# Row and key scores of an attention block issued as four 32-column matmuls each

## The chip, the core and the metric

The kernel runs on one core of a Trainium2 chip. The core has a matrix engine (PE, with its weight loads listed as PEld), a vector engine (DVE), a scalar engine (ACT), GpSimd (POOL), a queue engine for transfers (SP), and 16 DMA engines. The metric is the device time of the whole program in microseconds. Each time below is a median of runs or comes from one profiled execution.

## What is computed

One transformer block in float32: layer norm, attention with 16 heads of 8 dimensions over 8 sequences of 512 tokens, a residual, a second layer norm, and a feed-forward part with one shared and eight routed experts (two per token). The part that matters here is the attention:

```python
q = (x @ Wq.T + bq).reshape(b, s, HEADS, HEAD_DIM)        # b=8, s=512, 16 heads of 8
k = (x @ Wk.T + bk).reshape(b, s, HEADS, HEAD_DIM)
attn = jnp.einsum('bqhd,bkhd->bhqk', q, k) / np.sqrt(HEAD_DIM)
attn = jax.nn.softmax(attn, axis=-1) * head_mask[None, :, None, None]
out = jnp.einsum('bhqk,bkhd->bqhd', attn, v).reshape(b, s, HIDDEN)
```

## The kernel before

Heads are taken in groups of four (`hg`, 4 groups; `j` is the head in the group), and sequences in a loop (`b`, 8 of them: the first and the last are written out, the six between are a hardware loop). q and k are kept as bfloat16 parts, three for each value, so that a product of parts gives float32 accuracy. This is why a score contracts over 72 part rows and more, though a head has 8 dimensions.

Scores are computed twice. **Row scores** (`row_scores`, L1147) put 128 queries on PSUM partitions and 512 keys along the free axis. DVE takes the maximum over the keys of two such tiles at once (L792, four PSUM banks, so PE may be two pairs ahead). The maxima are split into parts and transposed by PE (`max_rows`, L1191), copied by ACT (L630) and sent by a small DMA (L314) into two extra rows of `q_op`. **Key scores** (`key_scores`, L1165) put 128 keys on partitions and 512 queries along the free axis. Their contraction runs over 128 rows, and the two extra rows subtract the maximum of each query. ACT takes the exponential of a whole tile (L643) into `probs`. The key scores have two banks (four in the last two groups of heads), so the key score of step n waits for the exponential of step n-2.

**The product** of probabilities and values (`pv`, L1176) follows 11 steps behind. It takes one tile of 128 keys at a time: four matmuls in float32, one for each head, each with 32 columns of weights and 512 queries. Head `j` writes PSUM partitions 32j to 32j+31 of one bank. In the trace a float32 matmul is two records, so a `pv` shows as 8 matmul records. It is the only place where the 128 columns of PE are used as four tiles of 32.

A group of heads has 16 steps `s`. Step s issues its key score (K) and zero to two row scores (R) of the group after next (`ROW_TILES`). With four steps to a `pv`, PE's order repeats as

K R, K R R, K R, K, pv

Four such periods make a group of heads, 16 a sequence and 128 the attention. Other work of PE is put in between at fixed steps: `max_rows` after step 7 of each group, the output projection of the sequence before (`project_out`, L1202, once each after steps 0 to 3 of group 1), a transpose of the normalised rows (L1215, group 2), the router (L1221, group 3) and the ranks of the routed tokens (L1232 to L1239, group 3). All of these use weights of 128 columns. After the attention, the experts take the rest of the time, from about 510 us on.

DVE has its own order: the maximum of a row pair, and between them the transposes and the norm of the group's output, the residual, statistics and routing.

## Time and profile before

| | us |
|---|---|
| time, median of 3 runs | 732.31 (731.01 to 732.35) |
| span of the profiled execution, first to last instruction | 730.6 |
| PE busy in it | 653.3 |
| DVE busy | 551.8 |
| ACT busy | 440.2 |
| one iteration of the loop over sequences (of the seven after b = 0) | about 55 |

The busy time of an engine is the time in which at least one of its instructions is recorded as running. PE's matmuls overlap: a matmul of 512 columns in bfloat16 is recorded with 380 ns, while the next one starts 220 ns after it. So the distance between the starts says what a matmul costs, and the recorded length adds the way through the array. A timeline row can merge several instructions (x8); its start is that of the first and its length reaches to the end of the last. An arrow in brackets names what ended the idle time before a row. "Idle" is only counted where no instruction of the engine is recorded. K stands for a row of L1165, R for one of L1147, and pv for one of L1176.

### The profile page before, as it was taken

The page shows a single profiled execution, that of the slowest core. Times are in us where ns is not written, and L with a number is a line of the kernel's source. Part 1 is how long each engine was busy: PE and PEld are TensorE (multiplying, and loading weights), DVE is VectorE, ACT ScalarE, POOL GpSimd, SP SyncE. Part 2 cuts the span into 40 slices and gives each one's busy share as a digit, 9 for nine tenths or more (in the row PEclk, how much of TensorE's full clock was granted, in tenths as well). Part 3 has the DMA queues.
Part 4 walks back from the last instruction along what each step waited for, and adds up shares of the span by engine and source line. Part 5 has one row for each costly group of instructions (what it writes and reads, how often), then busy time and mean ns, then how long its engine had stood idle before and what let it go on. Part 6 is the DMA issues. An engine that isn't in the chain of part 4 may idle for free.

```text
span 730.6 us, 15017 instructions
## 1 busy us (share of the span) xinstructions
PE 653.3 (89%) x3976; PEld 330.0 (45%) x3976; DVE 551.8 (76%) x1252; ACT 440.2 (60%) x953; POOL 241.6 (33%) x314
## 2 busy tenths in 40 slices
PE   2866899999899899899899899898788999999996
PEld 1531222332233223223223223223578999999965
DVE  6989799999699698698698698663165666666658
ACT  0870577786586586587587487486524555555541
POOL 6767000022221211311311310413374455545541
PEclk9995799999999899999999899899998999999999
DMA  5499575212112112212112212100022222222164
GB/s 144 123 333 322 132 187 167 49 51 59 51 42 64 54 33 71 56 33 69 58 33 69 58 33 57 37 2 17 14 59 63 67 65 65 65 65 65 47 224 137
DMA packets 67592, 61.04 MB, mean 84 GB/s; under 512 B 16250, under 2 KB 58106, under 8 KB 67562
## 3 DMA queue, kind: packets, MB, share of 16 engines
q1 hardware_dynamic: 63242, 51.79, 25.8%
q0 software_dynamic: 4320, 8.89, 3.6%
q8 instruction: 14, 0.23, 0.1%
q14 instruction: 16, 0.13, 0.1%
HBM read 35.76 MB, written 24.62 MB: 83 GB/s over the span
## 4 chain that ended last, share of the span: by engine, by line
PE 64%; DVE 11%; issue 9%; POOL 3%; ACT 1%; another core or an unknown queue 1%; DMA 1%; DVEq 0%; SPq 0%; ACTq 0%; POOLq 0%
PE ps L1165 14%; PE ps L1176 13%; PE ps L1147 11%; PE ps L1350 10%; PE ps L1362 9%; DVE mx L792 5%; POOL slots L501 2%; DVE x_sb L1090 2%; PE ps L1302 1%; PE ps L1310 1%; PE ps L1340 1%; PE ps L1202 1%; PE ps L1221 1%; ACT probs L643 1%
## 5 line engine op out<-in xcount | busy, mean ns | idle before, releaser
L643 ACT ACTIVATE probs<-ps 128x512 f32<-128x512 f32 x512 | 281.3, 595 | 131.1 <-PE ps L1165 105.4
L792 DVE TENSOR_REDUCE mx<-ps 128x2 f32<-128x1024 f32 x256 | 306.4, 1213 | 50.7 <-PE ps L1147 39.0
L1165 PE MATMUL ps<-q_op,k_op 128*128 128x512 bf16 x512 | 199.5, 396 | 21.3 <-issue 14.2
L1147 PE MATMUL ps<-k_op,q_op 96*128 96x512 bf16 x512 | 187.8, 406 | 14.9 <-DVE mx L792 9.5
L1165 PEld LDWEIGHTS ps<-q_op,k_op 128*128 128x128 bf16 x512 | 50.1, 99 | 205.1 <-ACT probs L643 140.5
L1176 PE MATMUL ps<-probs,v_op 128*32 128x512 f32 x1024 | 141.2, 626 | 0.0
L690 ACT ACTIVATE probs<-ps,b_cur 128x128 f32<-128x128 f32 x284 | 81.4, 368 | 73.7 <-PE ps L1350 54.9
L501 POOL DMA_INDIRECT slots<-route_sb,slot_u x64 | 66.5, 1038 | 119.5 <-DVE slot_u L884 102.4
L544 POOL DMA_INDIRECT results<-rest,row_id x71 | 73.3, 1032 | 73.6 <-DVE rest L1034 55.8
L1147 PEld LDWEIGHTS ps<-k_op,q_op 96*128 96x128 bf16 x512 | 50.2, 101 | 68.9 <-DVE mx L792 34.3
L1350 PE MATMUL ps<-xn,qk 128*128 128x128 f32 x568 | 79.5, 284 | 1.4 <-ACT probs L690 1.1
L1362 PE MATMUL ps<-k_op,probs 128*128 128x128 f32 x568 | 75.2, 275 | 0.0
L1350 PEld LDWEIGHTS ps<-xn,qk 128*128 128x128 f32 x568 | 70.5, 195 | 6.2 <-ACT probs L690 5.3
L1362 PEld LDWEIGHTS ps<-k_op,probs 128*128 128x128 f32 x568 | 69.2, 192 | 0.2 <-issue 0.2
L465 POOL COPY v_op<-v_all 128x128 f32 (+1 forms) x32 | 9.3, 309 | 89.6 <-PE ps L1176 89.6
L473 POOL TENSOR_TENSOR mean_d<-stats 128x4 f32<-128x4 f32 x8 | 1.6, 202 | 110.1 <-DVE stats L841 110.1
L811 DVE STREAM_TRANSPOSE o_t<-ps 128x512 f32<-128x512 f32 x32 | 22.7, 708 | 19.5 <-remote 11.0
L1176 PEld LDWEIGHTS ps<-probs,v_op 128*32 128x32 f32 x1024 | 20.6, 109 | 36.4 <-issue 29.0
L1027 DVE COPY xn<-ps 128x128 f32<-128x128 f32 x71 | 20.6, 290 | 21.6 <-PE ps L1340 14.0
L1034 DVE TENSOR_TENSOR rest<-ps,b_sb 128x128 f32<-128x128 f32 x71 | 20.2, 284 | 21.5 <-PE ps L1362 21.5
L669 ACT ACTIVATE probs<-ps,b_sb 128x512 f32<-128x512 f32 x32 | 21.1, 689 | 22.4 <-PE ps L1302 19.9
L1310 PEld LDWEIGHTS ps<-w_sb,probs 128*128 128x128 f32 x256 | 31.1, 201 | 2.1 <-issue 1.9
(135 smaller groups left out, 623.5 us busy)
## 6 DMA issues: line engine op xcount, KB each, us to landing
q_op<-q_scr SPq DMA_DIRECT2D x96, 96.0 KB
k_op<-k_scr SPq DMA_DIRECT2D x96, 96.0 KB
w_sb<-in_W SPq DMA_DIRECT2D x18, 256.0 KB, 4.4
probs<-slots SPq DMA_DIRECT2D x71, 64.5 KB
k_scr<-probs SPq DMA_DIRECT2D x16, 256.0 KB, 3.2
q_scr<-probs SPq DMA_DIRECT2D x8, 384.0 KB, 3.0
k_scr<-probs SPq DMA_DIRECT2D x8, 384.0 KB, 3.5
k_scr<-probs SPq DMA_DIRECT2D x16, 128.0 KB, 3.0
```

The costliest lines, as they stand in the source:

```text
L501: nc.gpsimd.indirect_dma_start(slots, bass.IndirectOffsetOnAxis(slot_u[:, K2 * i + k:K2 * i + k + 1], 0), y2[:, i, k, :], None).then_inc(s ...
L544: nc.gpsimd.indirect_dma_start(results, bass.IndirectOffsetOnAxis(row_id[:, v, h:h + 1], 0), r_tile[:, v, h, :], None).then_inc(s_res[v], 16)
L643: nc.scalar.activation(probs[:, i, j, :], ps[:, BK_S + j % key_banks(b, hg), :], ACT.Exp, scale=float(D) ** -0.5).then_inc(s_exp, 1)
L690: nc.scalar.activation(hid_tile[:, par, c, :], ps[:, BK_TU + 2 * par + c // 2, TR * (c % 2):TR * (c % 2 + 1)], ACT.Gelu_apprx_tanh, bias=b ...
L792: nc.vector.reduce_max(mx[:, slot % 2, 2 * p:2 * p + 2], ps[:, bank:bank + 2, :], AX.X).then_inc(s_max, 1)
L811: nc.vector.transpose(o_t[:, :, :].rearrange("p a c -> p (a c)"), ps[:, BK_O, :]).then_inc(s_ot, 1)
L1147: last = nc.tensor.matmul(ps[:, BK_A + a % 4, :], q_op[hg][0:SH, j, P * i:P * (i + 1)], k_op[hg][0:SH, j, :], start=True, stop=True)
L1165: nc.tensor.matmul(ps[:, BK_S + j % key_banks(b, hg), :], k_op[hg][:, j, P * i:P * (i + 1)], q_op[hg][:, j, :], start=True, stop=True).the ...
L1176: last = nc.tensor.matmul(ps[32 * j:32 * j + 32, BK_O, :], v_op[:, hg, i, j, :], probs[:, i, j, :], start=(i == 0), stop=(i == NT - 1))
L1310: last = nc.tensor.matmul(ps[:, DN0 + b % 2, C * i:C * (i + 1)], hid[:, b % 2, c, P * i:P * (i + 1)], w2_sb[:, E, c, :], start=(c == 0), s ...
L1350: last = nc.tensor.matmul(ps[:, BK_TU + 2 * par + c // 2, TR * (c % 2):TR * (c % 2 + 1)], w1_cur[:, v, P * c:P * (c + 1)], yT_tile[:, par, ...
L1362: last = nc.tensor.matmul(ps[:, BK_TD + par, C * h:C * (h + 1)], hid_tile[:, par, c, P * h:P * (h + 1)], w2_cur[v][:, c, :], start=(c == 0 ...
```

## The change

Both kinds of scores are issued as four matmuls in place of one. Each takes 32 of the 128 weight columns and writes 32 PSUM partitions of the same bank; all four read the same moving operand of 512 columns. Nothing else changes: the waits stand before the first of the four, the semaphore is raised by the last, and the order of the steps is as it was.

```diff
@@ row_scores
-                last = nc.tensor.matmul(ps[:, BK_A + a % 4, :], q_op[hg][0:SH, j, P * i:P * (i + 1)], k_op[hg][0:SH, j, :],
-                                        start=True, stop=True)
+                for c in range(P // 32):
+                    last = nc.tensor.matmul(ps[32 * c:32 * c + 32, BK_A + a % 4, :],
+                                            q_op[hg][0:SH, j, P * i + 32 * c:P * i + 32 * c + 32], k_op[hg][0:SH, j, :],
+                                            start=True, stop=True)
                 if a % 2:
                     last.then_inc(s_sa, 1)
@@ key_scores
-                nc.tensor.matmul(ps[:, BK_S + j % key_banks(b, hg), :], k_op[hg][:, j, P * i:P * (i + 1)], q_op[hg][:, j, :],
-                                 start=True, stop=True).then_inc(s_sb, 1)
+                for c in range(P // 32):
+                    last = nc.tensor.matmul(ps[32 * c:32 * c + 32, BK_S + j % key_banks(b, hg), :],
+                                            k_op[hg][:, j, P * i + 32 * c:P * i + 32 * c + 32], q_op[hg][:, j, :],
+                                            start=True, stop=True)
+                last.then_inc(s_sb, 1)
```

The 1,024 score matmuls (512 row, 512 key) become 4,096, each with a weight load of its own. Lines behind the first edit move down by two to five in the changed kernel (L1147 to L1148, L1165 to L1168, L1176 to L1181, L1191 to L1196, L1202 to L1207).

PE in the loop over sequences, from the last key score of group 0 on: the `pv` behind it, and the first steps of group 1 with the output projections (ps is PSUM; REGISTER_ALU and ISA rows compute the value of a wait). Before:

```order
L1165 MATMUL ps<-q_op,k_op 128x512
L1176 MATMUL ps<-probs,v_op 32x512 x4
L209 ISA
L1165 MATMUL ps<-q_op,k_op 128x512
L209 ISA
L1147 MATMUL ps<-k_op,q_op 128x512
L1202 MATMUL ps<-wo_sb,o_sb 128x128
L1165 MATMUL ps<-q_op,k_op 128x512
L1147 MATMUL ps<-k_op,q_op 128x512 x2
L1202 MATMUL ps<-wo_sb,o_sb 128x128
```

After:

```order
L1168 MATMUL ps<-q_op,k_op 32x512 x4
L1181 MATMUL ps<-probs,v_op 32x512 x4
L209 ISA
L1168 MATMUL ps<-q_op,k_op 32x512 x4
L209 ISA
L1148 MATMUL ps<-k_op,q_op 32x512 x4
L1207 MATMUL ps<-wo_sb,o_sb 128x128
L1168 MATMUL ps<-q_op,k_op 32x512 x4
L1148 MATMUL ps<-k_op,q_op 32x512 x8
L1207 MATMUL ps<-wo_sb,o_sb 128x128
```

Every row of scores is now a row of four 32-column matmuls (or eight, where two row scores follow each other), in the same place. Before, the `pv` was the only 32-column work between 128-column rows. Now the projections are the only 128-column work between 32-column rows.

The same engine, later in group 1, around step 7 with the transpose of the maxima. Before:

```order
L1165 MATMUL ps<-q_op,k_op 128x512
L1147 MATMUL ps<-k_op,q_op 128x512
L209 REGISTER_ALU
L1165 MATMUL ps<-q_op,k_op 128x512
L1191 MATMUL ps<-id_bf,mx_parts 128x128
L1171 REGISTER_ALU
L1176 MATMUL ps<-probs,v_op 32x512 x4
```

After:

```order
L1168 MATMUL ps<-q_op,k_op 32x512 x4
L1148 MATMUL ps<-k_op,q_op 32x512 x4
L209 REGISTER_ALU
L1168 MATMUL ps<-q_op,k_op 32x512 x4
L1196 MATMUL ps<-id_bf,mx_parts 128x128
L1176 REGISTER_ALU
L1181 MATMUL ps<-probs,v_op 32x512 x4
```

The transpose (L1191, now L1196) keeps its 128 columns and stands between the key score of step 7 and the `pv`, both of which have 32-column tiles now.

## Rows read from the trace of the kernel before

**Rows 1.** The page: the chain that ended last, shares by engine

```profile
PE 64%; DVE 11%; issue 9%; POOL 3%; ACT 1%; another core or an unknown queue 1%; DMA 1%; DVEq 0%; SPq 0%; ACTq 0%; POOLq 0%
```

**Rows 2.** Timeline of PE: start us, us, engine line op out<-in xcount

```profile
311.18 0.39 PE L1165 MATMUL ps<-q_op,k_op 128*128 128x512 bf16 x1
312.28 0.38 PE L1165 MATMUL ps<-q_op,k_op 128*128 128x512 bf16 x1
312.50 0.38 PE L1147 MATMUL ps<-k_op,q_op 96*128 96x512 bf16 x1
312.75 0.39 PE L1165 MATMUL ps<-q_op,k_op 128*128 128x512 bf16 x1
313.07 1.07 PE L1176 MATMUL ps<-probs,v_op 128*32 128x512 f32 x8
314.06 0.39 PE L1165 MATMUL ps<-q_op,k_op 128*128 128x512 bf16 x1
```

**Rows 3.** Timeline of ACT beside it, same columns

```profile
311.61 2.18 ACT L643 ACTIVATE probs<-ps 128x512 f32<-128x512 f32 x4 [0.63 <-PE ps L1165]
```

**Rows 4.** Timeline of PE: the last three products, back to back

```profile
503.34 2.78 PE L1176 MATMUL ps<-probs,v_op 128*32 128x512 f32 x24
```

**Rows 5.** The page's costliest groups: weight loads (PEld) of scores and product

```profile
L1165 PEld LDWEIGHTS ps<-q_op,k_op 128*128 128x128 bf16 x512 | 50.1, 99 | 205.1 <-ACT probs L643 140.5
L1176 PEld LDWEIGHTS ps<-probs,v_op 128*32 128x32 f32 x1024 | 20.6, 109 | 36.4 <-issue 29.0
```

**Rows 6.** Timeline of PE: an output projection between scores, and a transpose before a product

```profile
304.71 0.39 PE L1202 MATMUL ps<-wo_sb,o_sb 128*128 128x128 f32 x2
304.94 0.38 PE L1165 MATMUL ps<-q_op,k_op 128*128 128x512 bf16 x1
310.03 0.22 PE L1191 MATMUL ps<-id_bf,mx_parts 128*128 128x128 bf16 x1
310.18 1.07 PE L1176 MATMUL ps<-probs,v_op 128*32 128x512 f32 x8
```

**Rows 7.** Timeline of DVE in b = 4: rows with idle time

```profile
308.57 0.69 DVE L834 TENSOR_TENSOR x_sb<-ps,x_sb 128x512 f32 x1 [0.54 <-PE ps L1202]
318.53 1.23 DVE L792 TENSOR_REDUCE mx<-ps 128x2 f32<-128x1024 f32 x1 [0.39 <-PE ps L1147]
321.41 2.36 DVE L792 TENSOR_REDUCE mx<-ps 128x2 f32<-128x1024 f32 x2 [0.36 <-PE ps L1147]
330.52 1.23 DVE L792 TENSOR_REDUCE mx<-ps 128x2 f32<-128x1024 f32 x1 [0.72 <-PE ps L1147]
334.17 1.23 DVE L792 TENSOR_REDUCE mx<-ps 128x2 f32<-128x1024 f32 x1 [0.87 <-PE ps L1147]
```

**Rows 8.** Windows: stretch, its length, busy time (x instructions) of each engine

```profile
303.27:358.39 55.12, 50.93 (x292) 16.34 (x291) 46.22 (x79) 38.30 (x74) 12.38 (x23) 0.97 0.21 53
310.18:313.07 2.89, 2.89 (x19) 0.79 (x17) 2.89 (x8) 2.26 (x6) 0.00 (x0) 1.00 0.02 3
347.76:354.38 6.62, 3.40 (x19) 0.79 (x17) 3.10 (x5) 2.03 (x5) 5.10 (x6) 0.93 0.16 51
354.38:358.39 4.01, 4.01 (x18) 0.92 (x17) 2.48 (x5) 2.64 (x5) 0.47 (x2) 0.69 0.05 16
```

**Rows 9.** L1176 by source: duration ns min/median/max, single pvs, then three in a row

```profile
L1176 PE MATMUL ps<-probs,v_op x24: 592/604/617, 310.2 to 316.9; 128*32 128x512 f32 x24
L1176 PE MATMUL ps<-probs,v_op x24: 592/592/617, 503.3 to 505.5; 128*32 128x512 f32 x24
```

**Rows 10.** Windows, same columns: b = 0, and the last two groups of heads

```profile
109.89:133.37 23.48, 23.48 (x131) 6.39 (x130) 21.23 (x27) 17.61 (x35) 0.31 (x1) 1.00 0.51 141
484.14:503.30 19.16, 18.01 (x120) 5.38 (x119) 6.11 (x28) 18.11 (x38) 0.92 (x3) 1.00 0.01 1
```

**Rows 11.** DMA: instruction queue 8 (packets, MB, share), and a small transfer

```profile
q8 instruction: 14, 0.23, 0.1%
q_op<-mxT SPq DMA_DIRECT2D x64, 4.0 KB, 1.7
```

## The prediction

> **What bounds the kernel now.** The chain that ended last lies on PE for 64% [rows 1], and the table above has PE busy for 653.3 of 730.6 us, DVE for 551.8. Recorded matmuls overlap, so I went on to PE's timeline and read distances between starts. One period of the attention (eight scores and a pv) runs from the pv at 310.18 to the one at 313.07, 2.89 us [rows 2, 6]. Its parts:
> - pv to the first key score K0: 0.99 (313.07 to 314.06).
> - K0 to the last key score K3, seven scores: 1.57 (311.18 to 312.75).
> - K3 to pv: 0.32.
> - One score elsewhere costs 0.22 (312.28 to 312.50).
>
> Seven scores at 0.22 would be 1.54. K3 comes at 1.57 because it waits until the exponential of K1 has freed its bank: ACT starts 0.43 after K0 and runs four exponentials in 2.18, one behind the other [rows 3], so the second ends about 1.1 later, and 0.43 + 1.1 is K3's time.
>
> Then DVE: in 55.12 us, one iteration of the loop, it is busy for 46.22 [rows 8]. Of the 8.9 idle us about 5.0 lie in two windows (3.10 busy of 6.62, 2.48 of 4.01), where all engines stand still for a while (PE is busy for 3.40, ACT for 2.03 of the 6.62) and PE's granted clock falls behind it (0.93 and 0.69 on average, a mix of the levels 2.4 and 1.2 GHz) [rows 8]. Outside them DVE is over 90% busy, in places (the window from 310.18) without a gap [rows 8]. So PE and DVE take turns as the bound, and what PE gains is worth no more than DVE's idle time before a maximum or the residual: 0.54, 0.39, 0.36, 0.72, 0.87 and smaller ones [rows 7].
>
> **What the change removes: two turns of PE's shape per period.** K3 to pv takes 0.10 more than a score's 0.22. What a pv costs among its own kind is in the last three pvs, which follow each other: 24 records in 2.78 against 8 in 1.07, so (2.78 - 1.07)/4 = 0.43 for each of its two passes, 0.86 a pv [rows 4, 6]. In the period it holds PE for 0.99, 0.13 more. Going into and out of 32-column tiles thus costs 0.10 + 0.13 = 0.23 a period. With scores in the same tiles both go.
>
> The Trainium skill ("TensorEngine Tiling (Array Packing)", Tiling Modes) says that changing the tiling mode drains the engine, while changing the tile within a mode does not. The trace agrees, with the 0.10 and 0.13 above. By its sentence alone the change is a plain gain on PE.
>
> **What a tiled score costs.** No row shows a bfloat16 score in 32-column tiles. Lower bound: the 0.22 of a full one. Upper bound: the four run one after another, 0.88. The nearest row is pv, with the same four tiles: a pass takes 0.43 [rows 4], twice the 0.22 of bfloat16, as a float32 pass should if all four tiles run at once. Its operands need 512 x 4 bytes in 0.43 for each tile and partition, which is the rate of 512 x 2 in 0.22. What speaks for more is that records of single pvs are 592 or 617 ns long, half of each [rows 9]: a first pass takes 0.025 longer, a weight load that nothing hides. In the three pvs in a row the median is the minimum, 592, so it is paid once and not six times [rows 9]. Tiled scores follow each other in the same way. I take 0.22, and keep 0.22 + 0.025, about 0.25, for the range. ACT starts when the last of the four tiles is done, which I put at 0.02 later (an estimate from the same 0.025): K0 to K3 becomes 1.59.
>
> There are 3,072 more weight loads. One of 32 columns is recorded with 109 ns against 99 for a full one in bfloat16 [rows 5], and four of them are unseen beneath a pass of 0.43. Four beneath 0.22 is twice that rate.
>
> The Trainium skill ("TensorEngine Tiling (Array Packing)", Restrictions) says that column tiling disables the fast weight load, which speaks against the change. By "TensorE: Matmul & The Clock Gate" (LDWEIGHTS) a load takes its columns divided by 1.2 GHz; four of 32 are an estimated 0.107 us, still under 0.22. By the rule a score would cost more only where its load is exposed.
>
> **A plain period afterwards:** pv to K0 0.86, K0 to K3 1.59, K3 to pv 0.22. That is 2.67 for 2.89 (the parts of before sum to 2.88), so -0.21.
>
> **What the change adds: turns around 128-column work.** A projection between scores costs nothing but itself now (304.71 to 304.94, 0.23) [rows 6]. Afterwards it stands between tiled scores and pays both turns, +0.23. The same holds for the transposes and the router (one block each), whose periods come out even: +0.23 - 0.21. In a period with a max_rows, score to transpose is a new turn (+0.10), transpose to pv stays (0.15) [rows 6], pv to K0 gains 0.13: about even. Three projections fall in one period.
>
> **One iteration, followed on DVE.** DVE works without a gap until about 308.0, then waits for the fourth projection (0.54 idle) [rows 7]. While DVE has no gap it holds PE, and I take this to hide the first of the three projections between scores; the other two pay +0.46, K3 to pv gives 0.10 back: **+0.36**. From 309.3 to 318.1 DVE is the bound: 0. From 318 to 334 the idle times above are DVE waiting for row scores, 2.34 in the last four of [rows 7]. PE's lead grows by 0.23 at the first pv, 0.21 at four more and 0.02 at the one behind a max_rows, and loses 0.23 in two insertions: **-0.63**, which the gaps can take as it builds up. From 334 to 344 DVE is the bound again: 0. In the slow-clock stretch DVE is idle for 1.5 of 4.01 [rows 8]. No row prices a turn at the low clock; between 0.23 (the same) and 0.46 (twice), one and a half periods save 0.35 to 0.69. I take the lower end, as K3 there waits for ACT: **-0.35**. Sum -0.6. Six such iterations: **-3.7**.
>
> b = 0 with the group behind it has no inserts but max_rows: 16 periods, of which 12 save 0.21, -2.5. DVE is idle for 2.25 of the second half's 23.48 [rows 10] and as much in the first, so nearly all of it is taken: **-2.3**. The last sequence has no further row scores in its last two groups, and there ACT is busy 18.11 of 19.16 [rows 10]: 0. Its first two groups have the projections (+0.36) and some plain periods: **-0.5**. The row scores before 77 us and the experts: 0 (DVE and loads bound the first; the second is untouched).
>
> Sum -6.5: the profiled 730.6 becomes 724.1. The median lies 1.7 above that span, and becomes **725.8** (732.31 - 6.5).
>
> **Rivals.** (1) *DVE takes it.* If the gaps shrink less than I counted (another maximum is late, ACT is next), the six iterations give 0 and b = 0 gives -1: 731.3. For: DVE over 90% busy. Against: each gap is released by PE.
> (2) *Slower: the loop's code.* PE's loop body grows by 384 matmuls and 384 loads; one iteration now has 292 and 291 records [rows 8], so it becomes about 2.3 times as long. The instruction queue moved 14 packets of 16 KB [rows 11], and its share of 0.1% of 16 engines is some 11.7 us, 0.8 each; a small transfer takes 1.7 from issue to landing [rows 11]. If the longer body no longer stays in the engine, each of six jumps back waits 1.7 to 2.5 us for its first block: +10 to +15, less 6.5: 736 to 741. It decides once the body is larger than what is kept. Nothing in the rows shows where that is.
> The Trainium skill ("Runtime: NRT & Kernel Launch", Instruction fetch mechanics) gives PE room for 2,048 instructions in blocks of 256; the new body is some 1,470 by count, so it should fit, unless the blocks fetched ahead push its start out.
> (3) *Slower: loads or tiles in line.* If each tiled score costs 0.25, a period is 7 x 0.25 + 0.25 + 0.90 = 2.90 and nothing is gained, while eleven insertions an iteration (four max_rows, four projections, one each of transposes, router and ranks) pay 0.23 each. With DVE's own stretches hiding two thirds of these 2.5 us, that leaves +0.8, six times: 737. For: the 0.025 above, and the doubled rate of loads. Against: it appears once in three pvs.
> (4) *Much slower: no overlap* in bfloat16 or with one shared moving operand, 0.88 a score: +0.66 x 1,024, less DVE's slack, over 1,300 us. The rate of pv speaks against it.
>
> **How the numbers follow.** Chances: forecast 0.57, (1) 0.15, (2) 0.13, (3) 0.12, (4) 0.03. The forecast's own range is 719 to 729: at its low end twice the gain is taken (-13), at its high end half. The range must leave out no more than two in ten: 718 to 738 leaves out (4), the longer half of (2), and a little at both ends. A measurement of this kernel tells 0.2% (1.5 us) from no change. Faster by more: the forecast and a part of (1), 0.61. Within: 0.13. Slower: (2), (3), (4) less what they leave, 0.26.
>
> **What would show it.** In the profile after: distances of 0.22 from the first record of a score to that of the next (0.25 for rival 3), 0.22 from K3 to pv, 0.86 from pv to K0, a plain period of 2.67; projections 0.23 dearer; DVE's idle rows shorter, its busy share up. Rival 2 shows as idle PE right behind the jump back, once an iteration, and more packets on queue 8. I am wrong if weight loads are exposed at every score, or if the standstill once an iteration grows with PE's number of instructions.

## The result: slower by 2.4%, and the profile after

The changed kernel takes 749.37 us (median of 4 runs, 748.18 to 750.9) where the kernel before, measured beside it, takes 732.33 (731.01 to 733.71). The ratio is 1.024, 95% interval 1.021 to 1.028. The forecast was 725.8, with a range up to 738: the sign is wrong. The profiled execution spans 748.8 us where that of before spans 730.6.

The page of the kernel after, engines with busy time and number of instructions, then the chain that ended last and the instruction queue, as in [rows 1, 11]:

```profile
PE 649.5 (87%) x7048; PEld 351.7 (47%) x7048; DVE 551.4 (74%) x1252; ACT 440.4 (59%) x953; POOL 241.9 (32%) x314
...
q8 instruction: 23, 0.38, 0.2%
...
PE 58%; DVE 12%; issue 10%; POOL 3%; ACT 2%; another core or an unknown queue 2%; DMA 1%; DVEq 0%; SPq 0%; ACTq 0%; POOLq 0%
```

PE has 3,072 instructions more and is busy for 3.8 us less. The span grew by 18.2 us, so PE stands idle for longer.

Timeline of PE in the kernel after, the period that answers to [rows 2, 6] (start us, us, engine line op out<-in xcount):

```profile
320.08 0.23 PE L1196 MATMUL ps<-id_bf,mx_parts 128*128 128x128 bf16 x1
320.24 1.07 PE L1181 MATMUL ps<-probs,v_op 128*32 128x512 f32 x8
321.12 0.40 PE L1168 MATMUL ps<-q_op,k_op 128*32 128x512 bf16 x4
321.34 0.40 PE L1148 MATMUL ps<-k_op,q_op 96*32 96x512 bf16 x4
...
322.70 0.40 PE L1168 MATMUL ps<-q_op,k_op 128*32 128x512 bf16 x4
322.93 1.03 PE L1181 MATMUL ps<-probs,v_op 128*32 128x512 f32 x8
```

Here the forecast holds to within two hundredths of a microsecond. From the product to the first score there are 0.88 us, where it had 0.86, between two scores 0.22 (a group of four tiles moves on at the rate of one full-width matmul), from K0 to K3 1.58, from K3 to the product 0.23, and the period is 2.69 for 2.89, where it had 2.67.

Windows of the kernel after, columns as in [rows 8] (length, busy time and instructions of PE, PEld, DVE, ACT, POOL, then clock, DMA share, GB/s): one iteration of the loop, a plain period, and the two periods around the standstill.

```profile
312.54:370.48 57.94, 50.94 (x678) 18.93 (x674) 46.23 (x79) 38.37 (x74) 12.37 (x23) 0.94 0.20 50
320.24:322.93 2.69, 2.69 (x42) 1.09 (x45) 2.69 (x8) 2.06 (x6) 0.00 (x0) 1.00 0.02 3
...
357.95:367.44 9.49, 4.40 (x41) 1.09 (x44) 4.00 (x6) 3.01 (x6) 5.11 (x6) 0.68 0.13 43
367.44:370.48 3.04, 3.04 (x44) 0.97 (x40) 2.06 (x4) 1.96 (x5) 0.00 (x0) 0.88 0.00 0
```

The iteration takes 57.94 us where it took 55.12. The period with the standstill takes 9.49 us where it took 6.62 [rows 8]. PE works for 4.40 of them, at a granted clock of 0.68, a mix of the levels 2.4 and 1.2 GHz. In its fifth pair of numbers POOL is busy for 5.11 us, where the plain period has 0.00.

What every engine does there, in both kernels. Timelines of PE, ACT and POOL in the kernel before (in brackets the idle time just before):

```profile
348.76 0.39 PE L1165 MATMUL ps<-q_op,k_op 128*128 128x512 bf16 x1
...
352.44 0.39 PE L1165 MATMUL ps<-q_op,k_op 128*128 128x512 bf16 x1 [2.42 <-issue]
...
351.79 0.60 ACT L643 ACTIVATE probs<-ps 128x512 f32<-128x512 f32 x1 [3.19 <-remote]
353.19 0.60 ACT L643 ACTIVATE probs<-ps 128x512 f32<-128x512 f32 x1 [0.80 <-PE ps L1165]
...
344.58 1.10 POOL L501 DMA_INDIRECT slots<-route_sb,slot_u  x1 [14.03 <-DVE slot_u L884]
345.98 0.96 POOL L501 DMA_INDIRECT slots<-route_sb,slot_u  x1 [0.30 <-issue]
...
353.57 0.96 POOL L501 DMA_INDIRECT slots<-route_sb,slot_u  x1 [0.30 <-issue]
```

And in the kernel after:

```profile
356.40 0.39 PE L1168 MATMUL ps<-q_op,k_op 128*32 128x512 bf16 x4
...
357.45 0.40 PE L1168 MATMUL ps<-q_op,k_op 128*32 128x512 bf16 x4 [0.45 <-issue]
...
360.37 0.40 PE L1168 MATMUL ps<-q_op,k_op 128*32 128x512 bf16 x4 [1.36 <-issue]
360.60 0.39 PE L1148 MATMUL ps<-k_op,q_op 96*32 96x512 bf16 x4
364.62 0.62 PE L1168 MATMUL ps<-q_op,k_op 128*32 128x512 bf16 x4 [3.63 <-issue]
...
359.72 0.60 ACT L643 ACTIVATE probs<-ps 128x512 f32<-128x512 f32 x1 [2.32 <-remote]
363.97 0.60 ACT L643 ACTIVATE probs<-ps 128x512 f32<-128x512 f32 x1 [3.65 <-remote]
364.46 0.25 ACT L630 ACTIVATE mxT<-ps 32x128 bf16<-32x128 bf16 x1
...
354.02 1.10 POOL L501 DMA_INDIRECT slots<-route_sb,slot_u  x1 [13.82 <-DVE slot_u L884]
...
363.00 0.96 POOL L501 DMA_INDIRECT slots<-route_sb,slot_u  x1 [0.30 <-issue]
```

POOL issues the eight indirect scatters of put_rows, one every 1.26 us, 9.95 us in all. Some 4 us behind the first of them (3.4 in the kernel after) ACT begins to wait for key scores that PE's own record shows as done. In a free period an exponential starts 0.04 us behind the recorded end of its score (311.18 + 0.39, then 311.61) [rows 2, 3]. In the kernel before, the score of 348.76 ends at 349.15 and its exponential starts at 351.79, 2.6 us later. In the kernel after, the score of 356.40 ends at 356.79 and its exponential starts at 359.72, 2.9 us later; the score of 357.45 ends at 357.85, and its exponential starts at 363.97, 6.1 us later and just behind the last scatter (363.00 + 0.96).

Which exponential belongs to which score follows from the order of the program. A score waits for the exponential two scores back, as those of 352.44 and 364.62 do here, and the copy L630 at 364.46 stands right behind the exponential of step 7. PE in turn waits for these exponentials. So the standstill reads as a wait for PE's completion signals while POOL issues scatters, and time is already lost in the first sequence that has scatters beside it. That is a reading of two timelines; the runs below test it.

### The profile page after: what moved, and what is told of

Read it like the earlier page. It is cut to its first block, busy times and chain, and to the rows that moved or that the text cites. A ratio compares the mean times of both kernels' runs of the same rounds, so it can differ in the third digit from the quotient of the medians.

```text
span 748.8 us, 21161 instructions
## 1 busy us (share of the span) xinstructions
PE 649.5 (87%) x7048; PEld 351.7 (47%) x7048; DVE 551.4 (74%) x1252; ACT 440.4 (59%) x953; POOL 241.9 (32%) x314
## 3 DMA queue, kind: packets, MB, share of 16 engines
q0 software_dynamic: 4320, 8.89, 3.6%
## 4 chain that ended last, share of the span: by engine, by line
PE 58%; DVE 12%; issue 10%; POOL 3%; ACT 2%; another core or an unknown queue 2%; DMA 1%; DVEq 0%; SPq 0%; ACTq 0%; POOLq 0%
PE ps L1168 12%; PE ps L1148 10%; PE ps L1181 10%; PE ps L1355 10%; PE ps L1367 8%; DVE mx L792 6%; POOL slots L501 2%; DVE x_sb L1090 2%; ACT probs L643 2%; PE ps L1207 2%; PE ps L1307 1%; PE ps L1315 1%; PE ps L1345 1%; PE ps L1226 1%
## 5 line engine op out<-in xcount | busy, mean ns | idle before, releaser
L1168 PE MATMUL ps<-q_op,k_op 128*32 128x512 bf16 x2048 | 205.7, 397 | 39.4 <-issue 24.4
L1148 PE MATMUL ps<-k_op,q_op 96*32 96x512 bf16 x2048 | 194.4, 408 | 18.6 <-DVE mx L792 13.0
L1181 PE MATMUL ps<-probs,v_op 128*32 128x512 f32 x1024 | 136.4, 610 | 0.0
L1168 PEld LDWEIGHTS ps<-q_op,k_op 128*32 128x32 bf16 x2048 | 54.9, 96 | 165.5 <-ACT probs L643 91.6
L1148 PEld LDWEIGHTS ps<-k_op,q_op 96*32 96x32 bf16 x2048 | 55.2, 99 | 111.8 <-DVE mx L792 63.9
L501 POOL DMA_INDIRECT slots<-route_sb,slot_u x64 | 66.4, 1038 | 118.1 <-DVE slot_u L884 101.0
L1181 PEld LDWEIGHTS ps<-probs,v_op 128*32 128x32 f32 x1024 | 29.7, 111 | 14.7 <-issue 3.3
```

The lines of the kernel that those rows point to most:

```text
L501: nc.gpsimd.indirect_dma_start(slots, bass.IndirectOffsetOnAxis(slot_u[:, K2 * i + k:K2 * i + k + 1], 0), y2[:, i, k, :], None).then_inc(s ...
L1148: last = nc.tensor.matmul(ps[32 * c:32 * c + 32, BK_A + a % 4, :], q_op[hg][0:SH, j, P * i + 32 * c:P * i + 32 * c + 32], k_op[hg][0:SH, j ...
L1168: last = nc.tensor.matmul(ps[32 * c:32 * c + 32, BK_S + j % key_banks(b, hg), :], k_op[hg][:, j, P * i + 32 * c:P * i + 32 * c + 32], q_op ...
L1181: last = nc.tensor.matmul(ps[32 * j:32 * j + 32, BK_O, :], v_op[:, hg, i, j, :], probs[:, i, j, :], start=(i == 0), stop=(i == NT - 1))
```

## The experiments

Theory A: while POOL issues indirect DMAs one behind the other, PE gets only so many instructions completed (or their signals passed on), so the standstill grows with PE's number of instructions there. Rivals: B, column tiling costs time by itself; C, the scatters have no part in it; D, the faster stream of tiles arrives in another phase. Each run stood beside runs of the kernel before, from which its ratio comes. Where a run leaves the scatters out, its text on record says so. "Iteration" is the stretch of [rows 8, first row] in that kernel's own trace, from the second product of b = 4 to that of b = 5.

| run | us, median | ratio, 95% interval | iteration, us |
|---|---|---|---|
| before | 732.33 | | 55.12 |
| after | 749.37 | 1.024 (1.021 to 1.028) | 57.94 |
| e1 before, no scatters | 689.59 | 0.940 (0.937 to 0.944) | 50.21 |
| e2 after, no scatters | 687.85 | 0.939 (0.935 to 0.943) | 50.13 |
| e3 full-width in group 0 | 733.16 | 1.001 (0.998 to 1.003) | 56.56 |
| e4 before, halves | 746.82 | 1.019 (1.014 to 1.023) | 59.93 |
| e5 two tiles of 64 | 760.35 | 1.039 (1.036 to 1.041) | 61.73 |
| e6 before, spaced | 698.36 | 0.954 (0.951 to 0.956) | 50.22 |
| e7 after, spaced | 701.46 | 0.957 (0.953 to 0.961) | 50.92 |
| e8 before, plain DMAs | 690.99 | 0.944 (0.942 to 0.947) | 50.21 |
| e9 before, POOL adds | 699.57 | 0.957 (0.952 to 0.962) | 51.03 |
| e10 tiled in group 0 only | 748.91 | 1.024 (1.020 to 1.028) | 58.03 |
| e11 before, two bursts | 711.01 | 0.972 (0.968 to 0.976) | 53.10 |
| e12 spaced, tiles in b = 0 | 698.48 | 0.955 (0.950 to 0.959) | 50.2 |
| e13 before, 24 plain DMAs | 696.50 | 1.010 (1.008 to 1.011), see below | 50.2 |
| e14 after, spaced by 4 | 707.69 | 1.025 (1.023 to 1.027), see below | 54.06 |
| e15 after, again | 750.63 | 1.025 (1.020 to 1.030) | 58.27 |
| e16 as e13, again | 704.49 | 0.961 (0.957 to 0.965) | 50.2 |

Each set of runs had one chip to itself. In five sets the medians of the kernel before lay between 732.1 and 733.5 us; in the set of e13 and e14 it took 689.73 (7 runs, 688.9 to 691.05). That set is a finding of its own, told at its place.

The iterations of one trace differ where there is a standstill, so the last column is one sample. Taken from the row numbers of one sequence to those of the next (slot_u on DVE, the rows that the scatters wait for), the first five take 55.1 to 56.3 us in the kernel before (mean 55.7), 58.0 to 59.9 after (58.8), 55.1 to 56.6 in e3 (55.7), 58.0 to 58.5 in e10 (58.2), 55.5 to 59.8 in the halves (58.2) and 58.9 to 61.9 in e5 (61.1). Without the scatters they agree to 0.03.

**Is it the scatters? (e1, e2)**

```diff
-                for i in range(NT):
-                    for k in range(K2):
-                        nc.gpsimd.indirect_dma_start(slots, bass.IndirectOffsetOnAxis(slot_u[:, K2 * i + k:K2 * i + k + 1], 0),
-                                                     y2[:, i, k, :], None).then_inc(s_put, 16)
+                pool.sem_inc(s_put, 16 * NC)
```

> The kernel before, without the indirect scatters of the loop (put_rows raises its semaphore and issues nothing; the experts' tiles and the results are then read from rows written elsewhere, in the same number and size, so this part of the computation is left out). Theory A (PE's completion signals are passed on late while GpSimd issues the eight scatters, and the standstill of group 0 is that lateness): the standstill goes in the kernel before already. The two periods around it took 6.62 and 4.01 us where a plain one takes 2.89, so 4.8 us an iteration and, with the low clock behind it, 5 to 6: six of them take 730.6 to about 700 (695 to 706). Theory C (the standstill is owed to something else at that place, the shift copies, the loads or the loop's own code): 728 to 732, with the standstill where it was.

> The changed kernel without the same scatters (left out as in the run before it). Theory A: no standstill, so the tiles' own gain is left, 0.2 us in each plain period: below the kernel before without scatters by 6 to 10 us, some 690 to 696. Theory B (column tiles cost time by themselves at some places, with or without GpSimd at work): above the kernel before without scatters, by 10 us or more. Theory C: about 749, with the longer standstill.

Windows of e1, an iteration and the period that held the standstill, then the same of e2:

```profile
288.31:338.52 50.21, 49.24 (x292) 16.18 (x291) 46.00 (x79) 38.06 (x74) 4.53 (x15) 1.00 0.18 48
332.75:335.63 2.88, 2.88 (x18) 0.78 (x16) 2.66 (x4) 2.29 (x6) 0.00 (x0) 1.00 0.02 3
```

```profile
283.63:333.76 50.13, 48.66 (x679) 18.98 (x674) 46.10 (x79) 38.03 (x74) 4.53 (x15) 1.00 0.19 48
328.38:331.07 2.69, 2.69 (x42) 1.09 (x44) 2.49 (x3) 2.10 (x6) 0.00 (x0) 1.00 0.02 3
```

Theory C falls, and A had put e1 at 695 to 706, so more comes back than it counted. Without the scatters neither kernel has a standstill, and PE's clock stays at 1.00. The period that took 6.62 and 9.49 us takes 2.88 and 2.69. In spans of the profiled executions the scatters cost the kernel before 41.2 us (730.6 - 689.4) and the changed one 65.2 (748.8 - 683.6), 24.0 more. That overstates the growth: the profiled run of e1 is the longest of its four and that of e2 the shortest, and 4.3 of the 5.8 us between them lie ahead of the first row numbers (1.3 are a single wait for a copy's DMA in b = 0 that the profile of e1 has and that of e2 does not). From the row numbers of the first sequence to those of the seventh, the four traces take 327.2 us (before), 345.9 (after), 293.6 (e1) and 293.1 (e2). There the scatters cost 33.6 and 52.8 us, so the standstills grew by 19.3, and the tiles gained 0.6.

By medians the changed kernel is 17.0 us slower with the scatters and 1.7 us faster without them, and the medians of e1 and e2 cannot be told apart. So theory A's "6 to 10 us below" for e2 was too much. B falls for the loop: with 678 instructions for 292 an iteration takes 50.13 for 50.21.

Part of the 41 us lies behind the loop, where POOL issues its last scatters (L501 has 2% of the chain that ended last, on the page of before): from the last product to the end e1 takes 218 us and the kernel before 227.

**Which scores matter? (e3, e10)** Row scores of group 2 and key scores of group 0 are those issued in group 0 of a sequence, where the scatters run.

```diff
-                for c in range(P // 32):
+                w = P if hg == 2 else 32
+                for c in range(P // w):
```

This is row_scores of e3, with w for 32 in the lines below it; key_scores has `hg == 0`. In e10 the two widths are exchanged.

> The changed kernel, but the scores that are issued in group 0 of each sequence (row scores of group 2, key scores of group 0) are full-width as before; groups 1 to 3 are tiled. Theory A: in group 0, where the scatters run, PE has the instruction count of the kernel before, so the standstill is that of before (6.6 and 4.0 us in the two periods), while 48 of 64 periods keep the gain of 0.2 us where PE bounds them: 724 to 729. Theory B (the tiles themselves): between the two kernels, 740 to 746. Theory D (the faster stream of PE ahead of group 0 moves it against the scatters, and the phase makes the stall long): 745 or more, with the long standstill.

> The changed kernel with tiles only for the scores that are issued in group 0 of each sequence, where the scatters run; groups 1 to 3 are full-width as before. Theory A: group 0 alone carries the loss, so the long periods are those of the changed kernel (9.5 to 10.7 us and the one behind it 3 to 4.7), in spite of 48 of 64 periods being those of before: 745 to 752. Rival D (the stream of tiles ahead of group 0 decides): 730 to 736.

A quarter of the tiles carries the whole loss: e10 has them only beside the scatters and takes 748.91, the time of the changed kernel. e3 has them everywhere else and is within the noise of the kernel before (its 56.56 in the table is one of its long iterations; their mean is that of before). D falls with e10, B with e3. Theory A's 724 to 729 for e3 missed too: the tiles outside group 0 gain nothing that shows.

**Tiles, or the number of instructions? (e4, e5)**

```diff
-                last = nc.tensor.matmul(ps[:, BK_A + a % 4, :], q_op[hg][0:SH, j, P * i:P * (i + 1)], k_op[hg][0:SH, j, :],
-                                        start=True, stop=True)
+                for c in range(2):
+                    last = nc.tensor.matmul(ps[:, BK_A + a % 4, 256 * c:256 * c + 256], q_op[hg][0:SH, j, P * i:P * (i + 1)],
+                                            k_op[hg][0:SH, j, 256 * c:256 * c + 256], start=True, stop=True)
```

This is row_scores of e4; its key scores are cut alike. e5 is the changed kernel with 64 in the place of 32.

> The kernel before with every row and key score cut in two along its moving axis (two full-width matmuls of 256 columns each instead of one of 512): the same product with twice the score instructions and no column tiling. Theory A (number of instructions): the standstill grows by about a third of what four tiles add to it (one instruction more for each score where the tiles add three), so 735 to 742. Theory B (column tiling): 730 to 733, with the standstill of before, unless the second load of the weights shows (a load is 0.10 us beside 0.11 us of columns, so it should just be hidden).

> The changed kernel with two column tiles of 64 for each score instead of four of 32: the number of instructions of the halves (two for each score), as column tiles. Theory A (the standstill grows with PE's number of instructions, whatever their shape): the long periods of group 0 are those of the halves, 9.5 to 10.5 us, and the time is theirs, 747, or down to 742 for what shorter turns of shape give back. Theory B (four tiles in flight together are dear by themselves): about halfway from the kernel before to the halves or better, 733 to 740.

The halves use no column tiles at all, and the kernel before becomes 1.9% slower by them. The window with their standstill:

```profile
352.71:363.22 10.51, 3.90 (x27) 1.71 (x25) 3.48 (x6) 3.02 (x6) 5.54 (x7) 0.72 0.12 39
```

Their plain period still takes 2.89, so the loss is in group 0 again. The text of A missed its size: it put the growth at about a third of what the tiles add (735 to 742), and it is 13.7 us (746.82 against 733.10 beside it) where the tiles add 17.0, with twice the instructions of a score instead of four times. How PE stands in the last 6.44 us of the eight scatters shows what may be behind it. The groups of PE's matmuls there, by line (busy us, mean ns, idle before; the number of instructions is the x), in the kernel before (348.08 to 354.53), in the halves (353.02 to 359.46) and in the kernel after (357.52 to 363.96):

```profile
L1176 PE MATMUL ps<-probs,v_op 128*32 128x512 f32 x12 | 2.1, 757 | 0.0
L1165 PE MATMUL ps<-q_op,k_op 128*128 128x512 bf16 x4 | 1.8, 442 | 3.2 <-issue 3.2
L1147 PE MATMUL ps<-k_op,q_op 96*128 96x512 bf16 x4 | 1.4, 380 | 0.0
```

```profile
L1180 PE MATMUL ps<-probs,v_op 128*32 128x512 f32 x8 | 1.1, 605 | 0.0
L1148 PE MATMUL ps<-k_op,q_op 96*128 96x256 bf16 x6 | 1.0, 272 | 0.0
L1167 PE MATMUL ps<-q_op,k_op 128*128 128x256 bf16 x4 | 0.8, 278 | 1.5 <-issue 1.5
```

```profile
L1181 PE MATMUL ps<-probs,v_op 128*32 128x512 f32 x8 | 1.1, 604 | 0.0
L1168 PE MATMUL ps<-q_op,k_op 128*32 128x512 bf16 x8 | 0.8, 390 | 1.8 <-issue 1.8
L1148 PE MATMUL ps<-k_op,q_op 96*32 96x512 bf16 x4 | 0.4, 381 | 0.0
L1196 PE MATMUL ps<-id_bf,mx_parts 128*128 128x128 bf16 x1 | 0.2, 230 | 0.0
```

20, 18 and 21 matmuls (and 21 in e5 and in e10): PE gets through nearly the same number in the same time, whatever one of them is worth. That is some 4 for each scatter, where the windows of a free plain period count 19 in 2.89 us before [rows 8] and 42 in 2.69 after. These 20 hold eight scores in the kernel before, five in the halves, three in the kernel after. The same stretch of the other rows of scatters gives 20, 18 and 21 again in the four inner ones of the six up to 503 us; the first and the last of them let 28 to 33 through, and e3, full-width there, has 15 to 24 in the inner ones. The number is the same only in this stretch: over the whole row, 9.95 us, it is 38, 44 and 61, since 22, 30 and 44 pass in the first 3.5 us (matmuls under way at the boundary are counted on both sides). So "more instructions, longer standstill" is what the runs show; a fixed number for each scatter is a reading of one stretch.

The lateness can outlast the scatters. In the halves ACT starts the exponential of a score that ended at 354.16 only at 361.17, 7.0 us later and 1.7 us behind the end of the last scatter (358.50 + 0.96). That the halves, already stopped until then, leave four tiles little more to lose would explain why the two are so close; no run tests it.

e5 is slower than either, 760.35, where theory A had put it at 742 to 747. Its standstill (365.94 to 375.79, 9.85 us) is that of the others. Of the 3.8 us that its iteration has on that of the changed kernel, 2.1 are in the one period behind the standstill (5.14 us for 3.04), for which no cause was looked for. Most of the rest is in the other groups: a plain period takes 2.92, so tiles of 64 remove no turn of shape next to a product in tiles of 32, and the period with the projections takes 4.47 us (4.24 in the changed kernel, 3.66 before). A single mode for both was needed for the gain that the change has.

**Is it the transfers, the descriptors, or any work of POOL? (e8, e9)**

```diff
-                        nc.gpsimd.indirect_dma_start(slots, bass.IndirectOffsetOnAxis(slot_u[:, K2 * i + k:K2 * i + k + 1], 0),
-                                                     y2[:, i, k, :], None).then_inc(s_put, 16)
+                        nc.gpsimd.dma_start(slots[E * REGION - P * (K2 * i + k + 1):E * REGION - P * (K2 * i + k), :],
+                                            y2[:, i, k, :]).then_inc(s_put, 16)
```

That is e8. In e9 there stands in the place of the loop over the scatters:

```diff
+                for n in range(NC - 2):
+                    nc.gpsimd.tensor_tensor(busy_sb[:, n, :, :], y2[:, :, 0, 0:C], y2[:, :, 1, 0:C], ALU.add).then_inc(s_put, 16)
```

> The kernel before with the eight indirect scatters replaced by eight plain DMAs of the same rows to fixed rows, issued on GpSimd's queue too (the rows are not put at their slots, and experts' tiles and results are read from rows written elsewhere, in the same number and size; that part of the computation is left out). Theory P (what holds PE's signals is GpSimd making descriptors, for any DMA of its queue): a standstill of the kernel before in group 0, 720 to 733. Theory Q (it needs the indirect form, in which GpSimd reads 128 row numbers and makes 128 destinations): no standstill, 688 to 697.

> The kernel before with six additions of 512 columns on GpSimd, one behind the other, in the place of the eight scatters (that part of the computation is left out; the experts' tiles and the results are read from rows written elsewhere, in the same number and size). An addition of that size took GpSimd 1.27 us in the kernel before, so it is at work for 7.6 us without a pause. Theory A (it is the making of indirect DMAs on GpSimd that holds PE's signals): no standstill, every iteration 50.2 us as without scatters, 688 to 693. Rival G (any long stretch of GpSimd's work holds them): the long periods of group 0 come back, 715 or more.

In e8 the queue moves what it did before (4,320 packets, 8.89 MB in both pages), and the iteration takes 50.21: the transfers are innocent. POOL worked on the eight for 4.39 us, which is only just as long as it took until ACT's gap began in the kernel before, so e8 alone cannot tell the indirect form from any DMA of that queue. In e9 POOL adds without a pause for 6.35 us. Windows of e9, its iteration, and the periods ahead of and behind 334.12:

```profile
288.86:339.89 51.03, 49.24 (x292) 16.20 (x291) 46.80 (x79) 38.06 (x74) 10.83 (x21) 1.00 0.19 47
330.10:334.12 4.02, 3.07 (x19) 0.94 (x18) 4.02 (x5) 2.19 (x5) 4.02 (x5) 1.00 0.31 64
334.12:337.00 2.88, 2.88 (x18) 0.78 (x16) 2.65 (x4) 2.29 (x6) 2.19 (x3) 1.00 0.02 3
```

The period of the standstill is back at 2.88, so a busy POOL alone does not hold PE. The 0.8 us in the period ahead (4.02 for 3.20 in e1) have another cause: DVE's small subtraction L806 took 0.98 us there beside POOL's additions, where its median is 166 ns. Theory A's 688 to 693 missed. The rest of the 10 us above e1 is mostly POOL's additions behind the loop (from the last product to the end, 225 us for 218). Whether it takes the indirect form, or any DMA of that queue in a long enough row, took two more sets (e13 to e16, below).

**Does a pause help? (e6, e7, e11, e12)**

```diff
                     for k in range(K2):
+                        if not last and K2 * i + k:
+                            pool.wait_ge(s_exp, (b + 2) * (HG * J * NT) + 3 * (K2 * i + k))
+                            pool.sem_inc(s_go, 1)
                         nc.gpsimd.indirect_dma_start(slots, bass.IndirectOffsetOnAxis(slot_u[:, K2 * i + k:K2 * i + k + 1], 0),
```

This is e6 and e7. e11 waits ahead of the fifth scatter only, for 12 exponentials.

> The kernel before with its eight scatters of a sequence spread out: each but the first waits until ScalarE has made three more of its exponentials (about 2.2 us apart instead of 1.26 us, so GpSimd issues half of the time). Theory A1 (PE's signals pile up only while GpSimd issues without a pause, and are passed on in the pauses): most of the 41 us between the kernel before and its run without scatters comes back, 695 to 712. Theory A2 (each scatter holds PE's signals for a time of its own, wherever it stands): the same sum of waits, spread over six or seven periods, 725 to 735, unless the clock now stays up, which gives back some 10 us, 718 to 725.

> The changed kernel with the same spacing of the scatters. Theory A1: it loses its longer standstill, 695 to 712, and stands within 3 us of the kernel before with the same spacing. Theory A2: still above that one by 10 us or more, since there are more instructions of PE to pass in each scatter.

> The kernel before with its eight scatters in two bursts of four without a pause (5.0 us each), the second burst twelve exponentials (some 8.7 us) behind the start of group 0. In the kernel before ScalarE's first gap began 4.0 us behind the start of the first scatter. Theory A1 (the lateness builds up over an unbroken row of scatters and is gone in a pause): each burst of four holds ScalarE for at most about 1 us, so an iteration is 50.2 to 52 us and the time 698 to 710. Rival A2 (each scatter has its own price): as much as the eight in a row, over 720.

> A version that is meant to be the fastest: the scatters spaced as in the run of the kernel before with spacing (698.4 us), column tiles only in sequence 0, which has no instructions of 128 columns put in between (its 16 periods summed to 47.1 us full-width and 44.5 us with tiles), full-width from sequence 1 on. 698.4 - 2.6 = 695.8, range 694 to 699.

Windows of e6, as before the iteration and the period of the standstill; then the iteration of e7:

```profile
286.47:336.69 50.22, 49.25 (x292) 16.19 (x291) 45.99 (x79) 38.06 (x74) 12.35 (x23) 1.00 0.22 58
330.92:333.80 2.88, 2.88 (x18) 0.78 (x16) 2.65 (x4) 2.29 (x6) 1.00 (x2) 1.00 0.09 26
```

```profile
288.64:339.56 50.92, 49.16 (x678) 18.77 (x674) 46.09 (x79) 38.15 (x73) 12.38 (x23) 1.00 0.22 57
```

All eight scatters of an iteration are there, with 0.6 to 2.3 us between one and the next instead of 0.30 (after the first pair), and an iteration takes as long as without any. The last two of the eight rows of scatters, in the last sequence and behind it, are not spaced. PE's clock stays at 1.00. Two bursts of four keep a part of the loss: two periods of an iteration become 5.29 for 3.62 and 4.10 for 2.88, 2.9 us in all. That is more than A1 had put it at (an iteration of 50.2 to 52, 698 to 710 us; measured 53.10 and 711.01), so four in a row are already enough to hold PE. But the lateness grows with the length of the row and is gone in a pause, as A1 has it, and a price of its own for each scatter (A2) is out with e6. Spaced, the changed kernel is 3 us above the kernel before, not the 17 of the unspaced pair; its iteration keeps 0.8 us of waits in the periods ahead of and behind the old standstill.

e12 was meant to add the gain in b = 0 to that and measured no more than e6: 698.48 for 698.36. In its profile b = 0 takes 45.4 us for 47.1, so 1.7 of the 2.6 us are there, but less than the medians can tell. The best version is e6, the kernel before with the spacing: 4.6% faster than it, 6.8% faster than the changed one, with nothing changed on PE.

**A longer row of plain DMAs, and a chip without the standstill (e13 to e16)**

```diff
-                for i in range(NT):
-                    for k in range(K2):
-                        nc.gpsimd.indirect_dma_start(slots, bass.IndirectOffsetOnAxis(slot_u[:, K2 * i + k:K2 * i + k + 1], 0),
-                                                     y2[:, i, k, :], None).then_inc(s_put, 16)
+                for n in range(3 * NC):
+                        i, k = n % NC // K2, n % K2
+                        to = (E - n // NC) * REGION - P * (n % NC + 1)
+                        nc.gpsimd.dma_start(slots[to:to + P, :],
+                                            y2[:, i, k, :]).then_inc(s_put, 16)
```

This is e13 (e16 is the same kernel): 24 plain DMAs, and the waits on s_put raised with them. e14 is e7 with 4 for 3 exponentials, e15 the changed kernel itself.

> The kernel before with 24 plain DMAs of 128 rows in the place of the eight scatters (three times the transfers, to fixed rows; rows are not put at their slots, and that part of the computation is left out as in the run with eight). The eight took GpSimd 4.39 us in a row, and in the kernel before ScalarE's gap began only 4.0 us behind the first scatter, so eight were too short to show a lateness that builds up. 24 make a row of 13.2 us. If GpSimd's making of descriptors for any DMA holds TensorE's signals, the long periods of group 0 come back, 715 to 745 us. If it needs the indirect form, iterations are 50.2 to 51 us as with eight, and the time is 691 plus what the 16 more DMAs of each of the last two sequences add behind the loop (8.8 us each, part of it hidden): 695 to 710.

> The changed kernel with its scatters four exponentials apart instead of three (some 2.9 us). If its remaining 0.8 us of waits an iteration are late signals that want a longer pause, the iteration goes from 50.92 to 50.1 to 50.3 us and the time from 701.5 to 696 to 699, level with the kernel before spaced (698.4). If they have another cause (the copies and LayerNorm scales that stand behind the scatters on GpSimd's queue), they stay or grow: 700 to 706.

> The changed kernel once more, beside new runs of the kernel before, since in the last set the kernel before took 689.7 us where it had taken 731 to 733 in all others: the time that it takes without its scatters' standstill. If the standstill is a matter of the chip, two cases: where the kernel before takes about 732, the changed one takes about 749 again; where it takes about 690, there is no standstill to grow, and the changed kernel takes 684 to 690 (the tiles' own gain, 0 to 6 us). If the changed kernel's long standstill comes also where the kernel before has none, 705 to 750.

> The kernel before with 24 plain DMAs a sequence, once more (they took GpSimd 13 us in a row; rows are not put at their slots, and that part of the computation is left out). It decides only where the kernel before itself has the standstill (about 732): then, if any descriptors made by GpSimd hold TensorE, 715 to 745; if only the indirect form does, 695 to 698, as in the last set. Where the kernel before takes 690 it is 696 to 697 again and decides nothing.

e13 told nothing by itself, since the kernel before can hardly have had its standstill on that chip: it took 689.73 us with its scatters in a row, as much as e1 takes without them on another chip. That is read from the time alone; the kernel before was not profiled there, and one set cannot tell the chip from anything else that was different in it. e14 is slower there mostly for a reason of its own: its wide spacing makes the LayerNorm scales late, which stand behind the scatters on POOL's queue (in its profile ACT's L614 waits 2.29 us for POOL's L487). That is the second case of its text (700 to 706, measured 707.69); that the changed kernel's last 0.8 us in e7 are late signals is not shown by it.

e15 and e16 met a chip like the others. e15 repeats the result, 1.025. Timeline of POOL in e16:

```profile
327.06 12.84 POOL L503 DMA_DIRECT2D slots<-route_sb  x24 [13.81 <-DVE slot_u L886]
```

A row of 12.84 us, longer than the eight scatters' 9.95, and all periods are as in e1: 2.88 in the place of the standstill. With the kernel before at 733.47 beside it, it is the indirect form that is needed; GpSimd at work on plain DMAs for as long does not do it. The whole of e16 is 8 us longer than e13, the same kernel (704.49 and 696.50), and above the 695 to 698 of its text. Their loops agree to 0.1 us an iteration; the difference is behind the loop, from the last product to the end (234 us and 226). There 71 indirect scatters of results run beside the experts, but they do so in e8 too, which takes 219 us for that stretch on a chip with the standstill; what makes the 8 us was not tested.

## Why the prediction was wrong

- **Turns of shape (0.10 + 0.13 removed), a tiled score at 0.22, plain period 2.67: right.** Measured 2.69, 0.22 and 0.23. "TensorEngine Tiling (Array Packing)", Tiling Modes, in the Trainium skill speaks of a drain on changing the mode only; the plain period of e5, 2.92 with tiles of 64 beside products in tiles of 32, agrees. Rivals 3 and 4 are out by the same rows: a tiled score is not 0.25 and not 0.88.
- **Weight loads: right.** 3,072 more of them leave the distance of scores at 0.22.
- **Rival 2, the loop's code: slower it was, but not by this.** Queue 8 moved 9 packets more, but e2 carries the same long body and moves the same 23 packets with iterations of 50.13 to 50.15 us.
- **Insertions at +0.23: too low, and not hidden by DVE.** The period with three projections became 4.20 in e2 for 3.62 in e1. From a score to the projection and on to the next score it was 0.22 + 0.23; it is 0.74 (313.61 to 314.35 in the kernel after). That is 0.29 an insertion, and the first of the three costs as much as the others, where I had DVE hide it. Period by period (e1 and e2), seven plain ones are 0.19 to 0.23 shorter, 1.43 in all, and six with an insertion are 0.05 to 0.58 longer, 1.38 in all. So the loop's own change is -0.08 us an iteration (50.21 to 50.13), where the working had -0.6, and of this -0.35 was booked in the slow-clock stretch. Of the forecast of -6.5, the medians without scatters show -1.7. The -5.8 between the two spans is an upper bound, and most of it lies in and ahead of b = 0.
- **The standstill taken as fixed: the step that failed.** The working read its two windows [rows 8], subtracted them from DVE's idle time and carried them over at their old length, and even took a gain in the slow-clock stretch behind them. It named no cause for a stop of all engines once an iteration. POOL's 5.10 busy us stood in the same row of [rows 8], against 0.00 and 0.47 in the two others. The clause at the end ("or if the standstill once an iteration grows with PE's number of instructions") is what happened: from the row numbers of the first sequence to those of the seventh, the scatters cost 33.6 us before and 52.8 after. Against these 19.3 us more the tiles' own gain is small. With a cause looked for, this would have been a rival with a chance of its own, since the change takes PE from 292 to 678 matmuls an iteration. The lines on record then could not show that cause: it took the runs without scatters (e1, e2) and with them in other forms (e6, e16).
- **The clock** falls with it. The iteration's mean granted clock is 0.94 after, 0.97 before, and 1.00 without the standstill. If all that is missing is time at 1.2 GHz for 2.4, that is 2 x 0.06 x 57.94, about 7 us of the iteration at half speed, for some 3 before. How much of the longer iteration this makes, and how much the waits, was not separated.

What the change does on a chip like that of e13, where the kernel before seems to have no standstill, was not measured; with the growth of the standstill gone, the pair e1 and e2 suggests a gain of 2 us or so, which their medians cannot tell from none.

What also stays open is where PE's instructions wait. The profile has PE's matmuls done 2.6 to 7 us before ACT starts on them, which speaks for late signals; a profile that runs ahead of the engine would look the same. In every version each matmul comes with a weight load of its own, so the runs do not tell whether it is matmuls, loads or both that are held. Why the indirect form does this to PE is not shown. The number that passes, 18 to 21 matmuls in 6.44 us, is counted in windows that I set 3.5 us behind the first scatter, and what lets the first 3.5 us, and the first and last of the six rows, run more freely was not tested.

## What to carry to other kernels

Before a change that multiplies an engine's instructions is priced, every stretch in which all engines stand still needs a cause; an unexplained one is not a constant. Look then at the engine that is busy in it, here GpSimd in a row of indirect DMAs, and spread its work first: that gave 34 us here, where the change on TensorE had 2 (medians) to 6 to give. Run the kernel before beside every experiment, since what it loses can differ from one set to another by 6%. A split that keeps the engine's busy time the same need not be free: here both ways to cut a score into more instructions made the standstill longer.

## What the runs showed of the hardware that I had not expected

- While GpSimd issued indirect scatters of 128 rows, one every 1.26 us, TensorE was held little for some 3.5 us (22 matmuls full-width, 44 in tiles) and then got mostly 18 to 21 through in 6.44 us, with scores of one, two or four instructions (38, 44 and 61 over the whole 9.95 us). With plain DMAs of the same 8.89 MB, with 24 plain DMAs in a row of 12.84 us, or with GpSimd's additions for 6.35 us, the standstill was gone. Pauses of mostly 0.6 to 2.3 us between scatters were enough for the full-width kernel's loop to run as without them.
- This cost was not there in every set: the kernel before took 689.7 us on one of at least five chips, and 732.1 to 733.5 (medians) on the others, with a spread of under 10 us in each set.
- Four bfloat16 tiles of 32 columns, each with its own weight load, follow the next four at 0.22 us, the rate of one full-width matmul. An output projection of 128 columns between them costs 0.29 us more than between full-width ones.
- Beside GpSimd's additions of 512 columns a subtraction of 16 columns on VectorE took 0.98 us instead of 0.17.
